# Softmax sums by two wide matmuls, two key banks, and GpSimd instructions twice as wide in a convolution-attention, scan and expert kernel

## What is computed

```
x = x + Wo(softmax(q k^T / sqrt(128)) v)          # 4 images, 4096 tokens, 128 channels,
                                                  # q, k, v from a group norm of x
t = tokens(x)                                     # [4, 4096, 128]
kv = silu(ln(t) @ W_kv^T)                         # 8 heads of 128, k and v
s = q_proj . k ; m = cummax(s) ; e = exp(s - m)
t = t + mean over heads( cumsum(e * v) / cumsum(e) )
p = top-2 of softmax(ln(t) @ router_w + router_b), renormalised   # 8 experts
t = t + sum over experts( p_e * (ln(t) @ expert_w[e] + expert_b[e]) )
```

## Time and profile before

| | |
|---|---|
| median of 3 runs (lowest, highest) | 2713.94 us (2713.19 to 2719.81) |
| the profiled execution's own time | 2719.66 us |
| its span, first to last instruction | 2717.9 us |
| busy share of the span | PE 94%, DVE 79%, POOL 76%, ACT 68%, PEld 68% |
| mean granted TensorE clock | 0.983 of full |
| first part | about 1835 us |
| second part | about 883 us |

### The profile page before, as it was taken

How to read it: one execution, slowest core, us unless ns; L and a number is a source line. 1 busy time by engine, 2 the same in 40 slices (tenths; PEclk the granted TensorE clock), 3 DMA queues, 4 the chain that set the end, 5 groups by cost and what they waited for, 6 DMA issues and landing times. The chain is left out here.

```text
span 2717.9 us, 37024 instructions
## 1 busy us (share of the span) xinstructions
PE 2553.1 (94%) x10851; PEld 1856.2 (68%) x10851; DVE 2152.6 (79%) x3225; ACT 1840.3 (68%) x3375; POOL 2058.7 (76%) x1688
## 2 busy tenths in 40 slices
PE   6999999999999999999999999997889999999868
PEld 4888877788887788887778888773545555555433
DVE  6788887788887778888778978852888988888884
ACT  5667677676667766677766766765877777767540
POOL 4777777777776777777677777772558988989994
PEclk9999999999999999999999999998999999999899
DMA  1000000100000010000001000101445565555545
GB/s 66 9 9 9 13 12 9 40 8 13 12 9 9 8 41 15 9 9 12 9 13 32 9 12 13 47 8 53 171 172 218 186 240 214 213 204 196 227 173 198
DMA packets 58105, 198.38 MB, mean 73 GB/s; under 512 B 12752, under 2 KB 15376, under 8 KB 40496
## 3 DMA queue, kind: packets, MB, share of 16 engines
q1 hardware_dynamic: 57904, 196.03, 20.4%
HBM read 178.04 MB, written 17.96 MB: 72 GB/s over the span
## 5 line engine op out<-in xcount | busy, mean ns | idle before, releaser
L224 POOL TENSOR_TENSOR p_lo<-pf,p_hi 128x512 fp32r<-128x512 f32 x1024 | 1320.0, 1292 | 434.2 <-ACT p_hi L505 431.7
L500 ACT ACTIVATE pf<-s_ps 128x512 f32<-128x512 f32 x1024 | 612.8, 598 | 530.4 <-PE s_ps L376 529.3
L638 DVE TENSOR_REDUCE mx<-m_ps 128x1 f32<-128x512 f32 x1024 | 702.2, 687 | 296.1 <-PE m_ps L359 292.2
L654 DVE TENSOR_TENSOR sum_ps<-sum_ps,pf 128x512 f32<-128x512 f32 x960 | 661.6, 689 | 21.1 <-ACT pf L500 20.8
L505 ACT CAST p_hi<-pf 128x512 fp32r<-128x512 f32 x1024 | 627.2, 613 | 0.0
L374 PE MATMUL s_ps<-q_hi,kd_hi 128*128 128x512 f32 x1024 | 427.2, 417 | 0.0
L359 PE MATMUL m_ps<-w_both,q_hi 128*128 128x512 f32 x1024 | 403.6, 395 | 7.0 <-DVE mx L638 6.0
L388 PE MATMUL om_ps<-p_hi,v_hi 128*128 128x512 f32 x1024 | 401.3, 392 | 4.6 <-POOL p_lo L224 4.6
L376 PE MATMUL s_ps<-q_lo,kd_hi 128*128 128x512 f32 x1024 | 399.7, 390 | 0.0
L375 PE MATMUL s_ps<-q_hi,kd_lo 128*128 128x512 f32 x1024 | 399.6, 390 | 0.0
L389 PE MATMUL om_ps<-p_hi,v_lo 128*128 128x512 f32 x1024 | 399.1, 390 | 0.0
(11 more groups left out here) (205 smaller groups left out, 3481.0 us busy)
## 6 DMA issues: line engine op xcount, KB each, us to landing
bq<-weight_rows SPq DMA_DIRECT2D x64, 1024.0 KB, 6.3
gate_b<-gate_rows SPq DMA_DIRECT2D x64, 1024.0 KB, 4.8
xb<-in_x_dram SPq DMA_DIRECT2D x8, 1024.0 KB, 6.2
rb_sb<-inverse_rows SPq DMA_DIRECT2D x32, 256.0 KB, 3.9
tokens<-xb SPq DMA_DIRECT2D x32, 256.0 KB, 2.0
tp<-tokens SPq DMA_DIRECT2D x32, 256.0 KB, 5.4
rb<-norm_rows SPq DMA_DIRECT2D x32, 256.0 KB, 5.4
tv<-tokens SPq DMA_DIRECT2D x32, 256.0 KB, 5.5
```

Source lines behind the costliest of these rows:

```text
L224: nc.gpsimd.tensor_tensor(p_lo[:, r, :], pf[:, r, :], p_hi[:, r, :].bitcast(F32), ALU.subtract).then_inc(lo_done, 1)
L500: nc.scalar.activation(pf[:, g % RING, :], s_ps[:, g % 2, :], ACT.Exp, scale=SCALE).then_inc(exp_done, 1)
L638: nc.vector.tensor_reduce(mx[:, n % 2, sub, chunk:chunk + 1], m_ps[:, j % 2, :], AX.X, ALU.max).then_inc(m_max, 1)
L654: nc.vector.tensor_tensor(sum_ps[:], sum_ps[:], p, ALU.add).then_inc(sum_done, 1)
```

## The change

It does five things.

1. **Softmax sums.** For blocks 0 to 30, ACT casts `den` (`high_den`, tile 2), POOL takes the low part (`low_den`, between `low(2)` and `low(3)`), and PE multiplies both with a 128x128 of ones as float32r matmuls of 512 columns into `pj_ps`, in slot 5, or 6 in the first block of an image. DVE then multiplies with the identity (back into `den`), reduces to 128x4 and takes the reciprocal. `pj_ps` is free after the first of the three (`den_held`). `finish` moves from slot 10 to 14, and some one-off slots of blocks 27 and 30 move by 2 to 5. Block 31 keeps the old form.
2. **Key banks.** `k_ps` gets two banks, `mo_ps` keeps one. From piece 26 on every second piece sums in `v_ps[0]`. `expert_bias(f)` now waits for `output(f-1)`.
3. **Pairs on GpSimd.** `gated` makes two experts (1024 columns) per instruction into a ring of two pairs, `add_heads` two heads. A last instruction adds the two halves. `carried` copies the last column as before.
4. **Order.** `gated` stands in slots 4, 6, 0, 2, the experts in slots 6 to 12 (the last two together in slot 12, which is 4 of the next step), `output` in slot 4, `residual` in slot 2, `scaled` in slot 3, `square_out` in slots 3 and 4, the logits in slot 5.
5. **Tail.** From piece 25 on, the second and fourth pair of a piece are DVE's.

```diff
-        def den_slot(i):
-            return 1 if i == NB - 2 else 2
+        def den_slot(n):
+            return 6 if n % NB == 0 else 5
...
+            def low_den(n):
+                pool.wait_ge(den_h, n + 1)
+                nc.gpsimd.tensor_tensor(den_lo[:], den[:], den_hi[:].bitcast(F32), ALU.subtract).then_inc(den_l, 1)
...
             def denominators(n):
-                pe.wait_ge(sum_done, (n + 1) * KT)
...
+                elif n % NB == NB - 3 and n // NB + 1 < B:
+                    pe.wait_ge(k_diff, (n // NB + 1) * CK + 1)
...
+                if n < BLOCKS - 1:
+                    pe.wait_ge(den_l, n + 1)
+                    pe.matmul(pj_ps[:], ones_r[:], den_hi[:], start=True, stop=False)
+                    pe.matmul(pj_ps[:], ones_r[:], den_lo[:], start=False, stop=True).then_inc(den_pe, 1)
...
+            def high_den(n):
+                act.wait_ge(sum_done, (n + 1) * KT)
+                after(act, den_pe, n)
+                nc.scalar.copy(den_hi[:], den[:]).then_inc(den_h, 1)
...
-                nc.vector.reciprocal(rinv[:, n % 2, :], pj_ps[:, 0:QT]).then_inc(inv_done, 1)
...
+                nc.vector.tensor_tensor(blocks, pj_ps[:].rearrange("p (i c) -> p i c", i=QT),
+                                        ident[:].unsqueeze(1).to_broadcast([C, QT, C]), ALU.mult).then_inc(den_held, 1)
+                dve.wait_ge(den_held, n + 1)
+                nc.vector.tensor_reduce(dsum[:], blocks, AX.X, ALU.add).then_inc(diag_sum, 1)
+                dve.wait_ge(diag_sum, n + 1)
+                nc.vector.reciprocal(rinv[:, n % 2, :], dsum[:]).then_inc(inv_done, 1)
...
-    V_LAG, F_LAG, G_LAG, X_LAG = 5, 11, 3, 5
-    FREE = NBLK - (F_LAG - V_LAG)
+    V_LAG, F_LAG, G_LAG, X_LAG = 5, 11, 4, 6
+    FREE = NBLK - (F_LAG - V_LAG) - 1
...
-        k_ps = psum("k_ps", [C, BANK])
+        k_ps = psum("k_ps", [C, 2, BANK])
         row_ps = psum("row_ps", [C, BANK])
-        mo_ps = psum("mo_ps", [C, 2, BANK])
+        mo_ps = psum("mo_ps", [C, BANK])
...
+        def expert_slot(e):
+            return X_LAG + min(e, E - 2)
...
+                nc.gpsimd.tensor_tensor(xg[:, p % 2, :, :], gate_pair(f, p), twice(tv[:, f % NV, :]), ALU.mult).then_inc(xg_pool, 1)
+
+            def add_heads(v, part):
+                pool.wait_ge(y_dve, v * HEADS + 2 * part + 2)
+                if part == 1:
+                    after(pool, t2_dve, v)
+                    nc.gpsimd.tensor_tensor(acc[:], ay[:, 0:2, :], ay[:, 2:4, :], ALU.add).then_inc(y_pool, 1)
                 else:
...
+                    nc.gpsimd.tensor_tensor(acc[:], acc[:], ay[:, 2 * part:2 * part + 2, :], ALU.add).then_inc(y_pool, 1)
+
+            def add_halves(v):
+                pool.wait_ge(y_pool, v * YP + 4)
+                nc.gpsimd.tensor_tensor(acc[:, 0, :], acc[:, 0, :], acc[:, 1, :], ALU.add).then_inc(y_pool, 1)
...
-                after(pe, k_act, k * HEADS + h - (1 if two_banks(k) else 0))
+                after(pe, k_act, k * HEADS + h - 1)
```

More of the change, by code:

```diff
@@ L85, in softmax_attention @@
         nmax = sb("nmax", [C, 2, QT])
-        den = sb("den", [C, QB])
+        den, dsum = sb("den", [C, QB]), sb("dsum", [C, QT])
+        wv, wo, wvT = (den[:, i * C:(i + 1) * C] for i in range(3))
+        den_hi, den_lo = sb("den_hi", [C, QB], F32R), sb("den_lo", [C, QB], F32R)
         rinv = sb("rinv", [C, 2, QT])
@@ L245, in _ @@
                     low(g - 1)
+                if KT <= g < TILES and g % KT == 3:
+                    low_den(g // KT - 1)
                 if g < TILES and wrapped(g, GT + 2) is not None:
@@ L403, in denominators @@
                     pe.wait_ge(diff_dve, 1)
-                for i in range(QT):
-                    mm = pe.matmul(pj_ps[:, i:i + 1], den[:, i * C:(i + 1) * C], ones[:, 0:1], start=True, stop=True)
-                mm.then_inc(den_pe, 1)
+                if n < BLOCKS - 1:
+                    pe.wait_ge(den_l, n + 1)
+                    pe.matmul(pj_ps[:], ones_r[:], den_hi[:], start=True, stop=False)
+                    pe.matmul(pj_ps[:], ones_r[:], den_lo[:], start=False, stop=True).then_inc(den_pe, 1)
+                else:
+                    pe.wait_ge(sum_done, (n + 1) * KT)
+                    for i in range(QT):
+                        mm = pe.matmul(pj_ps[:, i:i + 1], den[:, i * C:(i + 1) * C], ones[:, 0:1], start=True, stop=True)
+                    mm.then_inc(den_pe, 1)
             pe.wait_ge(w_in, 160)
@@ L580, in _ @@
                         high_k(*wrapped(g, GT + 1))
+                    if n and t == 2:
+                        high_den(n - 1)
                     if n == 0 and t % GT == 1:
@@ L908, in key_bank, with spare_bank, sum_bank, by_vector @@
         def key_bank(k, h):
-            return v_ps[:, 1, :] if two_banks(k) and h % 2 else k_ps[:]
+            return k_ps[:, h % 2, :]
+        def spare_bank(f):
+            return f > FREE and (f - FREE) % 2 == 1
+        def sum_bank(f):
+            return v_ps[:, 0, :] if spare_bank(f) else mo_ps[:]
+        def expert_slot(e):
+            return X_LAG + min(e, E - 2)
         def turned():
             return st_ps[:].rearrange("p (g r) -> p g r", r=QUAD)
-        def by_vector(f, e):
-            return f >= FREE and e % 2 == 1
-        def vector_gated(f, e):
-            return max(f - FREE, 0) * (E // 2) + ((e + 1) // 2 if f >= FREE else 0)
-        def pool_gated(f, e):
-            return f * E + e + 1 - vector_gated(f, e)
+        def by_vector(f, p):
+            return f >= FREE and p % 2 == 1
+        def vector_gated(f, p):
+            return max(f - FREE, 0) * (PAIRS // 2) + ((p + 1) // 2 if f >= FREE else 0)
+        def pool_gated(f, p):
+            return f * PAIRS + p + 1 - vector_gated(f, p)
+        def pair_at(j, h):
+            f, p = (j - F_LAG, (h - G_LAG) // 2) if h >= G_LAG else (j - 1 - F_LAG, (h + HEADS - G_LAG) // 2)
+            return (f, p) if h % 2 == 0 and stage(f) else None
+        def gate_pair(f, p):
+            return gb[:, p // 2, 2 * (p % 2):2 * (p % 2) + 2, :]
+        def twice(t):
+            return t.unsqueeze(1).to_broadcast([C, 2, TOK])
         def rows_at(j):
@@ L1202, in _ @@
                         mean(norm1_at(j, 0))
-                    if norm2_at(j, 1) is not None and h == 3:
+                    if norm2_at(j, 1) is not None and h == 5:
                         logits(norm2_at(j, 1))
-                    if norm2_at(j, 1) is not None and h == 5:
+                    if norm2_at(j, 1) is not None and h == 6:
                         turn_logits(norm2_at(j, 1))
-                    if stage(f - 1) and h < X_LAG:
-                        expert(f - 1, E + h - X_LAG)
-                    if stage(f) and h >= X_LAG:
-                        if h == X_LAG:
-                            expert_bias(f)
-                        expert(f, h - X_LAG)
+                    if stage(f) and h == X_LAG:
+                        expert_bias(f)
+                    for e in range(E):
+                        if stage(f) and expert_slot(e) == h:
+                            expert(f, e)
+                        if stage(f - 1) and expert_slot(e) == h + HEADS:
+                            expert(f - 1, e)
                     if norm2_at(j, 2) is not None and h == 6:
@@ L1308, in _ @@
                         square_of_mean(norm1_at(j, 0))
-                    if norm2_at(j, 1) is not None and h in (1, 2):
-                        for b in (2 * h - 2, 2 * h - 1):
+                    if norm2_at(j, 1) is not None and h in (3, 4):
+                        for b in (2 * h - 6, 2 * h - 5):
                             square_out(norm2_at(j, 1), b)
-                    if norm2_at(j, 1) is not None and h == 4:
+                    if norm2_at(j, 1) is not None and h == 5:
                         hold_logits(norm2_at(j, 1))
@@ L1485, in _ @@
                 for h in range(HEADS):
-                    if stage(f - 1) and h < G_LAG and by_vector(f - 1, E + h - G_LAG):
-                        gated(f - 1, E + h - G_LAG)
-                    if stage(f) and h >= G_LAG and by_vector(f, h - G_LAG):
-                        gated(f, h - G_LAG)
-                    if stage(f - 1) and h == X_LAG:
+                    pair = pair_at(j, h)
+                    if pair is not None and by_vector(*pair):
+                        gated(*pair)
+                    if stage(f - 1) and h == expert_slot(E - 1) - HEADS:
                         output(f - 1)
```

175 lines of the change are left out of this document (84 added, 91 removed).

## The result

The changed kernel takes **2687.8 us** (median of 4 runs, 2687.0 to 2693.2) beside 2715.8 us for the kernel before on the same chip: ratio 0.9894, 95% interval 0.9879 to 0.9910, so 24 to 33 us less. The forecast was 2689.

The account below looks back on a forecast made before the run. PE was taken as the bound, with POOL and DVE close in the second part. First part -4, middle -18 and end -3 sum to -25: 2694.7 from the profiled 2719.7, so 2689 for the median of 2713.9; range 2655 to 2712.

Parts of the forecast that it names:

- The middle, -18: Second part with keys, values and experts all running: a group of four steps falls from 98 to 94 us, -18 us.
- Two thirds of PE's idle time: Middle of the second part: the share of PE's 6.6 idle us per group taken as gained, giving 94 us.
- Rival 1: PE's floor: all PE idle time in the middle goes and no seventh-block waits come; 2664 us, chance 0.13.
- GpSimd's pairs: Middle: 1024 columns take 2.42 us by a line through two sizes; POOL falls to 84.7 us per group.
- DVE beside POOL: Middle: DVE instructions sitting out a POOL instruction wait twice as long, about 3 us per group; DVE comes to 87.
- The 96 us: Group time if, by the skill's exclusion rule, a randomly arriving L1388 waits over 1 us on average; 96 instead of 94.
- Rival 3: Slower: DVE sits out whole wide GpSimd instructions, 94 us busy per group, group 101; 2734 us, chance 0.13.
- The first part, -4: Softmax attention: cheaper sums -14, POOL's lateness +1.4 and +1.5, shared bank waits +7; -4 us in sum.
- two tiles between users of this bank: Seventh blocks of three images: two-tile spacing in `pj_ps` costs PE waits of 0.8 and 1.5 us, 7 us in all.
- The upper end of +9: Softmax attention's worst case: POOL's 0.5 us comes in every block and `finish` collides with the group norm's steps.
- The first eleven steps, 0: Start of the second part: no gain, because these steps have two key banks in part already.
- The end: From 2509 to 2648 us -3 (between -10 and +4); last 70 us of experts alone 0, plus or minus 4.

Follow-up runs that it names:

- second_old: The changed kernel's first part (softmax attention) joined with the second part of the kernel before: 2707.4 us, ratio 0.9961 to the kernel before.
- old_slots: The changed kernel with residual, squares, logits and their turning back in the slots of the kernel before: 2734.8 us, ratio 1.0061.
- narrow: The changed kernel with every GpSimd instruction of 1024 columns written as two of 512 in the same places: 2692.4 us, ratio 0.9909.
- The two probes: The changed kernel with two more 16-column DVE instructions in slots 3 and 5, one with a PSUM input, one with both in SBUF: 2711.9 us, ratio 0.9983.
- first_old: The first part of the kernel before joined with the changed kernel's second part: 2697.0 us, ratio 0.9924 to the kernel before.
- seventh_slot6: The changed kernel with the softmax sums of the three seventh blocks in slot 6 instead of 5: 2693.2 us, one run.
- one_key_late: The changed kernel with two key banks for the first five steps and one from there on: 2707.4 us, ratio 0.9966.

## Why the prediction was right

**The middle, -18: right in size, and its causes are the named ones, in other shares.** The group came to 93.9 us for the forecast 94. "Two thirds of PE's idle time" was a guess between bounds, and one with the right reason: waits trade. That its number was met is in part luck. PE's idle time fell from 6.9 to 4.4 us per group, by little more than a third. The other 2.2 us are PE's busy time, 91.7 before and 89.5 after over four groups, which the forecast left at 91.4, its lower end. The granted clock was 0.98 before and 1.00 after. `second_old`, at 0.99, has 90.6 busy and 7.2 idle, so about half of the difference in busy time lies in the one profile of before.

The runs now show the rate of trade. 4.6 us of waiting for the key bank are worth 2.6. The gates' 1.2 are worth 0.4. 5 us more on DVE cost 2.3. One term was too small: for the single `mo_ps` bank the prediction allowed 0.6 us at most, and PE now waits 1.3 us per group for DVE's output (5.1 in four groups), where the kernel before has no such wait. What the prediction had wrong is the role of the slots. It costed the later squares as a wait of 1.9 us that goes (1.4 per group over all four). They and the residual's slot are worth 6.7 us per group against the old slots, because the pairs make the end of the scan late. That is part of the price of pairs, and without the new slots the change would have lost (`old_slots`, 1.0061). Rival 1 wanted all of PE's idle time gone, and 4.4 us of it are left.

**GpSimd's pairs: right.** The line through two sizes gave 2.42 us, and 1024 columns take 2.39. POOL came to 84.0 for 84.7. `narrow` shows that this bought nothing on PE in the middle, as argued.

**DVE beside POOL: the mechanism held, the doubling did not.** DVE came to 85.2 for 87. The residual's median is 1.35 us where the prediction wanted less than 1.2. It had taken the residual's wait as 0.16 us from the median. By the mean of four groups the wait was 0.41 us and is now 0.69. The successor of L1455 was to take 2.4 us and takes 0.15:

```profile
L1506 DVE TENSOR_SCALAR share<-share x8: 148/149/676, 2011.2 to 2632.5; 128x16 f32<-128x16 f32 x8
```

Another instruction of 16 columns took its place, L1460 (L1409 before), whose median rose from 0.43 to 1.62 us, 2.1 in the group shown. So the place in the order decided here which instruction sat out GpSimd, and doubling every wait was no measure of it. The Trainium skill, "SBUF — State Buffer", section "Who interferes with whom", says that a VectorE instruction with two SBUF inputs contends with a GpSimd instruction that reads SBUF, and that one with at most one SBUF input, outside the two-port modes, does not. The two probes show this line. The 96 us that the prediction worked out by this page did not come. It took arrivals as random and a wait of over 1 us. In the kernel after 5 of 16 residuals meet an idle GpSimd, the longest wait is 1.7 us, and the mean is the 0.69.

**Rival 3** would have needed DVE at more than 92 us per group, and it stayed at 85. With the probes it is 90, and the group is 96.2.

**The first part, -4: right in sign, 2.5 us too small.** Its errors went both ways. The saving per ordinary block is 0.36 us, not 0.46 (-11.2 in 31 blocks for -14), because the new sums cost 0.53 us. POOL's lateness in ordinary blocks, costed at 1.4 us in all, is 0: PE has no gap there. In the first blocks of three images the wait for `p_lo` in slot 6 is 0.48 us, forecast 0.5, and the wait for `v_lo`, which was to stay, is gone. Block 0, which has no sums ahead of it, took 0.9 us longer, but so it did in `first_old`, which has the old first part, so this is not the sums' doing. In block 26 the wait for row maxima rose from 0.4 to 1.0 us, and block 31 has a new one of 0.4 us for POOL's `den_lo`. The prediction had seen neither. And in each seventh block one new wait came (0.81 us, forecast 0.8) but not the second of 1.5 us. The failed step is the rule "two tiles between users of this bank", taken for both places. The user ahead of the second place is the sums, whose bank DVE frees with one product (0.68 us), not with a cast and a difference behind ACT. `seventh_slot6` shows that its limit lies between one tile and two. The upper end of +9 was summed too low as well: POOL's 0.5 us in every block and a collision of `finish` together come to +13.

**The first eleven steps, 0: wrong, -4.4.** The step was "have two key banks in part already". Two banks served keys 0 to 4 alone; with values from step 5 on, the kernel before had one. `one_key_late` has the stretch back at 139.6 us, so these 4.4 us are the key bank's (139.0 before, 138.3 in `second_old`).

**The end.** -3 and 0 were forecast. v = 23 to v = 31 gave -4.4, together with two steps that belong to the middle, and all behind it -0.2. The last pieces follow each other in 9.1 us instead of 8.4, as in the chain of the kernel after:

```profile
2653.38 2.37 POOL xg L1094
...
2655.79 1.04 PE mo_ps L1238 x2
...
2656.90 4.69 DMA gate_b<-gate_rows
2661.59 0.85 issue
2662.44 2.37 POOL xg L1094
```

The term took the pairs and PE's use of them as one loop and the DMA as hidden. The chain shows them one behind the other: the DMA, 0.9 us till GpSimd starts, a pair, PE's first two experts, the next DMA. In the kernel before the last three outputs stand 9.1, 8.7 and 8.5 us apart, in `second_old` 7.4, 9.3 and 7.1. So the steady piece is longer now, by some 0.3 to 1.2 us. Whether the whole tail is, the traces leave open (91.3 to 95.9 us with the new one, 89.8 and 91.5 with the old), and it lies within the 4 us that the prediction gave this term.

## What to carry to other kernels

When three engines are each busy for nine tenths, a wait in the list is not its worth. Here two removed waits gave back a third and a little over a half of their lengths, and work added to DVE cost PE about a half. Part of that came as busy time of PE at another granted clock. So compare PE's busy time and its idle time apart, before and after: a sum can fit while neither does. Grouping instructions moves the end of what is grouped, so its readers have to move by slots too. Here this was worth more than the grouping and the freed PSUM bank together. When a second user comes between two users of one PSUM bank, count for each the chain up to its own release, not the distance in tiles.

## What the runs showed of the hardware

The exclusion of DVE and GpSimd works both ways in this trace. Timeline of the kernel after, DVE and POOL:

```profile
2210.01 2.40 POOL L1094 TENSOR_TENSOR xg<-gate_b,tv 128x1024 f32<-128x1024 f32 x1
2210.41 1.28 DVE L1433 TENSOR_TENSOR_SCAN ay<-ay,carry,v_ps 128x512 f32<-128x512 f32 x1
2211.61 1.35 DVE L1440 SCALAR_TENSOR_TENSOR tv<-acc,tv 128x512 f32<-128x512 f32 x1
2212.36 1.75 POOL L1082 TENSOR_TENSOR xf<-tp,rb 128x512 f32<-128x512 f32 x1
...
2237.38 1.26 DVE L1408 TENSOR_TENSOR_SCAN u_r<-e_r,u_r,zeros 128x512 f32<-128x512 f32 x1
2237.54 3.29 POOL L1100 TENSOR_TENSOR acc<-ay 128x1024 f32<-128x1024 f32 x1 [0.24 <-DVE ay L1433]
2238.67 3.35 DVE L1414 RECIPROCAL b_r<-u_r 128x512 f32<-128x512 f32 x1
```

The residual waits till L1094 ends at 2212.4, then runs for 0.55 us, and L1082, next on GpSimd, has 1.75 us instead of 1.29 because it waits for that. The two take turns. The scan L1408, with both inputs in SBUF, holds L1100 up by 0.9 us, while the reciprocal behind it, with one input, runs beside GpSimd. And the scan with one of its inputs in PSUM (L1433) took 1.28 us in every one of 128 places of the four groups, beside a running L1094 too, as at 2210.41.
